# A routed expert layer: 32 experts over all tokens, against 39 (expert, tile) products over tokens sorted by expert

## The reference

```python
def _L2_ffn_ref(x, weight, scale, expert_masks, router_w):
    B, S, D_IN, D_OUT, E = (4, 128, 256, 256, 32)
    ...
    probs = jax.nn.softmax(jnp.einsum('bsd,ed->bse', x, router_w), axis=-1)
    top1_w, top1_idx = jnp.max(probs, axis=-1), jnp.argmax(probs, axis=-1)
    w_scaled = jnp.clip(jnp.round(weight / THRESH), -1.0, 1.0) * scale[:, None]
    def body(out, inputs):
        e_idx, mask_e = inputs
        y = jnp.einsum('bsi,oi->bso', x, w_scaled * mask_e)
        out = jnp.where((top1_idx == e_idx)[..., None], y * top1_w[..., None], out)
```

## Time and profile before

| | us |
|---|---|
| median of 3 runs | 1933.21 |
| lowest, highest | 1932.28, 1936.13 |
| the profiled execution, its time | 1934.06 |
| its span in the trace | 1932.3 |
| sublayer of the change: first router matmul to the first instruction of the epilogue | 1467.3 to 1608.2 |

### The profile page before, as it was taken

One profiled execution on the slowest core, in us unless ns is written; L12 is line 12 of the kernel. 1 busy time (PEld: TensorE's weight loads), 2 busy tenths in 40 slices (PEclk: granted clock), 3 DMA queues, 4 the chain that ended last, 5 costly groups with the idle time before them and its releaser, 6 DMA issues. The chain is left out here.

```text
span 1932.3 us, 32081 instructions
## 1 busy us (share of the span) xinstructions
PE 1599.6 (83%) x11620; PEld 1183.9 (61%) x11667; DVE 1422.6 (74%) x2379; ACT 790.1 (41%) x1245; POOL 529.3 (27%) x594
## 2 busy tenths in 40 slices
PE   7899999999898985566767678899995998889853
PEld 6678888887884662122546345688874884746631
DVE  3399999998666846899486764566685994668698
ACT  3367676666242635333234212533341002525522
POOL 2234444442342411776022003200000331314100
PEclk9899999999898987788969789999997999899975
DMA  3000000000000000000100020000001220010000
GB/s 148 28 28 27 27 27 26 23 27 6 12 1 13 3 8 36 0 0 0 47 4 2 28 109 4 12 18 12 12 19 57 74 65 31 2 58 2 2 1 22
DMA packets 18145, 49.24 MB, mean 25 GB/s; under 512 B 2035, under 2 KB 8436, under 8 KB 16886
## 3 DMA queue, kind: packets, MB, share of 16 engines
q1 hardware_dynamic: 18038, 47.78, 7.3%
HBM read 46.73 MB, written 1.05 MB: 25 GB/s over the span
## 5 line engine op out<-in xcount | busy, mean ns | idle before, releaser
L2124 DVE SCALAR_TENSOR_TENSOR arena<-psum,arena 128x1016 f32<-128x1016 f32 (+2 forms) x240 | 303.5, 1265 | 35.5 <-ACT arena L2061 29.8
L902 DVE TENSOR_REDUCE limits<-psum 128x4 f32<-128x512 f32 (+2 forms) x256 | 148.1, 620 | 81.9 <-PE psum L757 49.3
L1970 PE MATMUL psum<-ssm_XT_hi,ssm_split 128*128 128x512 f32 x640 | 194.2, 406 | 11.7 <-POOL ssm_split L1929 5.7
L870 ACT ACTIVATE PT<-psum 128x1024 f32<-128x1024 f32 x112 | 108.6, 1021 | 115.0 <-PE psum L788 115.0
L1970 PEld LDWEIGHTS psum<-ssm_XT_hi,ssm_split 128*128 128x128 f32 x640 | 115.9, 191 | 36.8 <-POOL ssm_split L1929 10.9
L2061 ACT ACTIVATE arena<-psum,arena 128x1024 f32<-128x1024 f32 x80 | 89.2, 1115 | 105.4 <-PE psum L1970 104.0
L2547 PE MATMUL psum<-expert,x 128*128 128x256 f16 x1024 | 114.0, 275 | 16.7 <-POOL expert L2533 16.7
L757 PE MATMUL psum<-K,QR 32*128 32x256 f32 (+1 forms) x320 | 118.3, 441 | 9.0 <-DVE limits L902 6.4
L2724 POOL TENSOR_TENSOR fed<-dtx,b_all 128x1024 f32<-128x1024 f32 x32 | 103.2, 3244 | 65.0 <-DVE state L2793 33.4
L2547 PEld LDWEIGHTS psum<-expert,x 128*128 128x128 f16 x1024 | 101.1, 99 | 29.5 <-issue 16.8
L2560 DVE SCALAR_TENSOR_TENSOR acc<-psum,gate_now,acc 128x256 f32<-128x256 f32 x256 | 111.9, 484 | 7.7 <-PE psum L2547 7.6
(11 more groups left out here) (443 smaller groups left out, 3850.0 us busy)
## 6 DMA issues: line engine op xcount, KB each, us to landing
expert_mask<-in_expert_masks SPq DMA_DIRECT2D x32, 256.0 KB, 2.6
arena<-in_ssm_in SPq DMA_DIRECT2D x16, 384.0 KB, 3.1
arena<-in_L_xattn SPq DMA_DIRECT2D x1, 5120.0 KB, 15.0
arena<-in_ssm_in SPq DMA_DIRECT2D x16, 256.0 KB, 3.0
arena<-in_L_ffn SPq DMA_DIRECT2D x1, 2592.0 KB, 9.0
arena<-in_L_xattn SPq DMA_DIRECT2D x2, 1280.0 KB, 9.5
arena<-in_L_ffn SPq DMA_DIRECT2D x1, 2176.0 KB, 8.2
ssm_gated<-in_ssm_z SPq DMA_DIRECT2D x4, 512.0 KB, 5.8
```

Of the source, the lines that this page charges most:

```text
L870: nc.scalar.activation(PT[:, u % 2, 2 * k:2 * k + 2, :, :].rearrange("p r h q -> p (r h q)"), p.psum[:, (2 + 2 * k) * 512:(4 + 2 * k) * 51 ...
L902: ins = nc.vector.tensor_reduce(limits[:, u % 2, r, :, k], score_bank(r)[:, :].rearrange("p (h k) -> p h k", h=4)[:, :, lo:hi], AX.X, ALU. ...
L1970: ins = nc.tensor.matmul(bank[tile_bank(r, tile) + half][:, :], w_part(tile, kw, c), x_part(kx, c, slice(half * 512, (half + 1) * 512)), s ...
L2124: ins = nc.vector.scalar_tensor_tensor(out[:, :, ago:], product[:, :, :P - ago], tap, out[:, :, ago:], ALU.mult, ALU.add)
```

## The change

The function is written anew; the rest of the program only moves by some lines. All is one block now.

The routing ends in a one-hot matrix (token x expert). Two matmuls over it count, for each tile and expert, the tokens up to each token and in all (the constants up_to and ones); a running sum over the counts (tensor_tensor_scan) gives each token its position among the tokens sorted by expert. Comparing these positions with 0 to 1023 gives a permutation matrix in float16, 8 tiles of 128 x 1024. TensorE multiplies the tokens by it: 8 x 8 matmuls of 128 x 512, which fill all 8 banks with the sorted, transposed tokens. ScalarE and VectorE copy four banks each to SBUF.

A sorted tile of 128 tokens holds only a few experts. Walking through sorted tokens, each step goes on either to the next expert or to the next tile, so 32 + 8 - 1 = 39 (expert, tile) pairs are enough. VectorE computes the list of pairs (finished, expert_at, index). In each step TensorE and VectorE read two numbers of the list from SBUF into registers (value_load) and use them as addresses. TensorE does 4 matmuls of 128 x 256 into one of four banks, VectorE adds the bank, times a 0/1 mask of the rows that belong to the pair, to the sum of that tile.

In the end the sum is split into two float16 parts again (ScalarE copies, VectorE subtracts), and 128 matmuls of 128 x 256 with the transposed permutation turn it back to the tokens' order. For that matrix, TensorE spreads the positions over the partitions (8 matmuls with ones, on a diagonal matrix that VectorE makes), ScalarE copies them out, and VectorE compares one tile after each fourth of the first 32 steps. VectorE then multiplies by probability and scale and adds to the tokens.

SP's loop over the masks is in the first block and starts right behind the next sublayer's weights. GpSimd multiplies the 32 masks one after the other, waiting for masks and for the ternary weight alone, and all 32 experts stay in SBUF. The sublayer's weights have two new tables, 0 to 1023 on all partitions and the row numbers.

```diff
--- before.py
+++ after.py
@@ -196,7 +196,8 @@
-        return [("router", rows(i[pre + "router_w"].T)), ("weight", rows(i[pre + "weight"].T)), ("scale", everywhere(i[pre + "scale"]))]
+        return [("router", rows(i[pre + "router_w"].T)), ("weight", rows(i[pre + "weight"].T)), ("scale", everywhere(i[pre + "scale"])),
+                ("positions", everywhere(np.arange(T, dtype=np.float32))), ("slots", np.arange(T, dtype=np.float32).reshape(B, P).T)]
...
@@ -2435,142 +2436,215 @@
...
-                with pe.Fori(0, trips) as i:
-                    for r in range(4):
-                        e = i * 4 + r
-                        pe.wait_ge(s.expert_ready.sem, s.expert_ready.at(e))
-                        for b in range(B):
-                            pe.wait_ge(s.product_taken.sem, s.product_taken.at(e * B + (b - B)))
-                            for part in range(2):
-                                for c in range(DC):
-                                    ins = nc.tensor.matmul(bank[b][:, :D], x16[:, part, c, b * P:(b + 1) * P], expert[:, r % 2, c, :],
-                                                           start=(part == 0 and c == 0), stop=(part == 1 and c == DC - 1))
-                            ins.then_inc(s.product_ready.up(trips), 1)
...
+    STEPS = E + B - 1
...
+            for e in range(E):
+                if e >= RING:
+                    sync.wait_ge(s.expert_ready.sem, s.expert_ready.at(e - RING))
+                sync.dma_start(mask[:, e % RING, :].rearrange("p (c n) -> p c n", c=DC), p.dram["expert_masks"][e]
+                               ).then_inc(mask_loaded[e % RING].up(16), 16)
...
+            pool.wait_ge(s.ternary_ready.sem, s.ternary_ready.at(0))
+            for e in range(E):
+                landed = mask_loaded[e % RING]
+                pool.wait_ge(landed.sem, landed.at(e // RING * 16 + 15))
+                nc.gpsimd.tensor_tensor(experts[:, e, :, :].rearrange("p c n -> p (c n)"), ternary[:, :], mask[:, e % RING, :], ALU.mult
+                                        ).then_inc(s.expert_ready.up(), 1)
...
+            pe.wait_ge(s.onehot_ready.sem, s.onehot_ready.at(0))
+            onehot = logits[:, :, :].rearrange("p b e -> p (b e)")
+            nc.tensor.matmul(bank[1][:, :B * E], p.c("up_to"), onehot, start=True, stop=True)
+            nc.tensor.matmul(bank[2][:, :B * E], p.c("ones"), onehot, start=True, stop=True).then_inc(s.counts_ready.up(), 1)
+            hold_clock(p, bank[7], 12)
+            pe.wait_ge(s.x16_ready.sem, s.x16_ready.at(1))
+            for b in range(B):
+                pe.wait_ge(s.perm_ready.sem, s.perm_ready.at(b))
+                for n, (part, c, half) in enumerate(tiles):
+                    ins = nc.tensor.matmul(bank[n][:, :], x16[:, part, b, c * P:(c + 1) * P], perm[:, b, half * 512:(half + 1) * 512],
+                                           start=(b == 0), stop=(b == B - 1))
+                    if b == B - 1:
+                        ins.then_inc(s.sorted_ready.up(), 1)
+            pe.wait_ge(s.diag_ready.sem, s.diag_ready.at(0))
+            pe.wait_ge(s.sorted_out_act.sem, s.sorted_out_act.at(3))
+            pe.wait_ge(s.sorted_out_dve.sem, s.sorted_out_dve.at(3))
+            for b in range(B):
+                ins = nc.tensor.matmul(bank[4 + b // 4][:, b % 4 * P:(b % 4 + 1) * P], p.c("ones"), diag[:, b, :], start=True, stop=True)
+            ins.then_inc(s.pos_psum.up(), 1)
+            pe.wait_ge(s.index_ready.sem, s.index_ready.at(0))
+            for i in range(STEPS):
+                e = pe.value_load(index[0:1, 0, i:i + 1], min_val=0, max_val=E - 1)
+                k = pe.value_load(index[0:1, 1, i:i + 1], min_val=0, max_val=B - 1)
+                pe.wait_ge(s.expert_ready.sem, s.expert_ready.at(min(i, E - 1)))
+                if i >= 4:
+                    pe.wait_ge(s.product_taken.sem, s.product_taken.at(i - 4))
+                for part in range(2):
+                    for c in range(DC):
+                        ins = nc.tensor.matmul(bank[i % 4][:, :D], sorted_x[:, bass.ds(k, 1), part, c, :].rearrange("p o t -> p (o t)"),
+                                               experts[:, bass.ds(e, 1), c, :].rearrange("p o n -> p (o n)"),
+                                               start=(part == 0 and c == 0), stop=(part == 1 and c == DC - 1))
+                ins.then_inc(s.product_ready.up(), 1)
...
+            pe.wait_ge(s.perm_turned.sem, s.perm_turned.at(B - 1))
...
+            for j in range(B // 2):
+                for half in range(2):
+                    b = 2 * j + half
+                    for k in range(B):
+                        for part in range(2):
+                            ins = nc.tensor.matmul(bank[4 + j][:, half * D:(half + 1) * D], perm[:, k, b * P:(b + 1) * P], acc16[:, part, k, :],
+                                                   start=(k == 0 and part == 0), stop=(k == B - 1 and part == 1))
+                ins.then_inc(s.y_ready.up(), 1)
...
+            nc.scalar.copy(x16[:, 0, :, :], p.X[:, :, :]).then_inc(s.x16_ready.up(), 1)
...
+            act.wait_ge(s.pos_psum.sem, s.pos_psum.at(0))
+            nc.scalar.copy(pos_row[:, :], p.psum[:, 4 * 512:6 * 512]).then_inc(s.pos_ready.up(), 1)
+            act.wait_ge(s.product_taken.sem, s.product_taken.at(STEPS - 1))
+            nc.scalar.copy(acc16[:, 0, :, :], acc[:, :, :]).then_inc(s.sum_split.up(), 1)
...
+            dve.wait_ge(s.x16_ready.sem, s.x16_ready.at(0))
+            nc.vector.tensor_tensor(x16[:, 1, :, :], p.X[:, :, :], x16[:, 0, :, :], ALU.subtract).then_inc(s.x16_ready.up(), 1)
...
+            then(nc.vector.tensor_copy(counts[:, :, :], bank[2][:, :B * E].rearrange("p (b e) -> p e b", b=B)))
+            then(nc.vector.tensor_tensor_scan(flat(cum), p.c("ones")[:, 0:1].broadcast_to([P, E * B]), flat(counts), 0.0, ALU.mult, ALU.add))
+            then(nc.vector.tensor_tensor(flat(base), flat(cum), flat(counts), ALU.subtract))
...
+            then(nc.vector.tensor_reduce(pos[:, :], chosen[:, :, :], AX.X, ALU.add))
...
+            for b in range(B):
+                nc.vector.tensor_scalar(perm[:, b, :], iota16[:, :], pos[:, b:b + 1], None, ALU.is_equal).then_inc(s.perm_ready.up(), 1)
+            for b in range(B):
+                ins = nc.vector.tensor_scalar(diag[:, b, :], p.c("ident"), pos[:, b:b + 1], None, ALU.mult)
...
+            then(nc.vector.tensor_tensor(finished[:, :, :], over_first(last_step[:, :], STEPS), over_last(positions[:, :STEPS], E), ALU.is_lt))
+            then(nc.vector.tensor_reduce(expert_at[:, 0, :], finished[:, :, :], AX.X, ALU.add))
...
+            nc.vector.tensor_copy(index[:, :, :], expert_at[:, :, :]).then_inc(s.index_ready.up(), 1)
...
+            for n in (1, 3, 5, 7):
+                dve.wait_ge(s.sorted_ready.sem, s.sorted_ready.at(n))
+                nc.vector.tensor_copy(sorted_tile(n), by_tile(n)).then_inc(s.sorted_out_dve.up(), 1)
...
+            for i in range(STEPS):
+                k = dve.value_load(index[0:1, 1, i:i + 1], min_val=0, max_val=B - 1)
+                at = dve.value_load(index[0:1, 2, i:i + 1], min_val=0, max_val=B * E - 1)
+                dve.wait_ge(s.product_ready.sem, s.product_ready.at(i))
+                if i:
+                    dve.wait_ge(s.product_taken.sem, s.product_taken.at(i - 1))
+                total_of = acc[:, bass.ds(k, 1), :].rearrange("p o n -> p (o n)")
+                nc.vector.scalar_tensor_tensor(total_of, bank[i % 4][:, :D], flat(chosen)[:, bass.ds(at, 1)], total_of, ALU.mult, ALU.add
+                                               ).then_inc(s.product_taken.up(), 1)
+                if i % 4 == 3 and i // 4 < B:
+                    if i == 3:
+                        dve.wait_ge(s.pos_ready.sem, s.pos_ready.at(0))
+                    nc.vector.tensor_scalar(perm[:, i // 4, :], pos_row[:, :], slots[:, i // 4:i // 4 + 1], None, ALU.is_equal
+                                            ).then_inc(s.perm_turned.up(), 1)
+            dve.wait_ge(s.sum_split.sem, s.sum_split.at(0))
+            nc.vector.tensor_tensor(acc16[:, 1, :, :], acc[:, :, :], acc16[:, 0, :, :], ALU.subtract).then_inc(s.sum_split.up(), 1)
...
+                dve.wait_ge(s.y_ready.sem, s.y_ready.at(j))
+                for half in range(2):
+                    ins = nc.vector.scalar_tensor_tensor(scaled[:, half, :], bank[4 + j][:, half * D:(half + 1) * D], top[:, 2 * j + half:2 * j + half + 1],
+                                                         p.w("scale"), ALU.mult, ALU.mult)
+                then(ins)
+                two = p.X[:, 2 * j:2 * j + 2, :]
+                then(nc.vector.tensor_tensor(two, two, scaled[:, :, :], ALU.add))
```

More of the change, by code:

```diff
@@ L2442, in masked_experts @@
     nc, s, bank = p.nc, p.s, p.bank
-    E = 32
+    E, RING = 32, 4
+    STEPS = E + B - 1
     mask_loaded = (s.mask_loaded0, s.mask_loaded1, s.mask_loaded2, s.mask_loaded3)
-    with ExitStack() as ctx:
+    with ExitStack() as ctx, nc.Block(no_gpsimd_drain=True) as block:
```

(32 more changed lines are left out.)

153 lines of the change are left out of this document (69 added, 84 removed).

## The result

The changed kernel takes 1947.1 us (median of 5 runs, 1944.07 to 1949.24), the kernel before 1932.32 (5 runs, 1931.79 to 1936.13): the ratio is 1.0073, with a 95% interval of 1.0059 to 1.0087. It is slower by 14.8 us, where 7 us less were forecast. The profiled execution took 1948.91, with a span of 1947.1.

The account below looks back on a forecast made before the run. PE and DVE were taken to bound the old loop together. Preparation 33 plus port 29 (62), loop 49.5 and end 22.5 gave a sublayer of 134 against 140.9 us, so 1926 us; 8-in-10 range 1892 to 1955.

Parts of the forecast that it names:

- preparation, undisturbed: From the router's first matmul to the first listed product, with no port waits: 33 us.
- the shared port: In the preparation, DVE instructions wait for GpSimd's running product: 29 us added, lower end 0, upper end 33.
- 39 listed products: The loop: 39 steps of 1.27 us on PE, 49.5 us, with 0.35 per register load.
- end: After the loop: splitting the sum, 128 matmuls turning back, last scalings and addition, into the epilogue: 22.5 us.
- the part on the loop: PE's step as two loads at 0.35, register instructions 0.37 and matmul issue 0.2: 1.27 us.
- The first rival: In the preparation the port costs little, 0 to 12 us instead of 29; 1897 to 1909 us, chance 0.2.
- The second rival: Register loads bound the loop by round trips, 0.67 us each; step 1.9, loop 74, 1951 us; chance 0.28.
- The third rival: Loop loads as cheap as register instructions, 0.05 to 0.15 us; step 0.67 to 0.87, 1903 to 1911 us; chance 0.12.
- DVE's step beside PE's: In the loop DVE's step is as long as PE's and runs beside it; PSUM waits cost nothing.
- The signs named ahead: Trace marks: GpSimd product spacing, slowed small DVE instructions, first listed product near 62, products 1.27 apart, slow-clock turning back.
- The case that came: Slower kernel: register loads bound the loop's 39 steps, sublayer 159 us, 1951 us; chance 0.28.
- its likeliest case: Port at full price in the preparation, loop loads of 0.25 to 0.43 us: 1926, range 1918 to 1933, chance 0.35.

Follow-up runs that it names:

- E1: The changed kernel with GpSimd waiting to start its 32 products until the list of steps is ready; 1926.94 us, ratio 0.9965 to the kernel before.
- E2: The changed kernel without the range checks of the values loaded into registers, loads kept; 1923.51 us, ratio 0.9938 to the kernel before.
- E8: The changed kernel with GpSimd's 32 products replaced by fills with ones that read nothing, masks left out; 1927.74 us, one execution.
- E4: The changed kernel with each step's pair from a fixed list known at build, no loads or checks; 1899.78 us, ratio 0.9817 to the kernel before.
- E6: E1 with one packed number loaded per step and taken apart in registers, no checks; 1896.72 us, ratio 0.981 to the kernel before.

## Why the prediction was wrong

Counted from the router's first matmul, forecast and measured:

| stretch | forecast | measured | difference |
|---|---|---|---|
| preparation, undisturbed | 33 | 32.4 (E1) | -0.6 |
| the shared port | 29 | 23.2 (changed kernel less E1) | -5.8 |
| 39 listed products | 49.5 | 76.5 | +27.0 |
| end | 22.5 | 22.9 | +0.4 |
| sublayer | 134 | 155.0 | +21.0 |

1926 and 21 are 1947. The step that failed is in the part on the loop: "on PE 2x2 behind the loads and 4 before the matmuls, at 0.046 0.37", and "With 0.2 for the matmuls' own issue". The number of instructions was right, their price not. The row 0.046 is of SP's additions to one register, an instruction of one kind, and its duration without the gaps to its neighbours. Measured: 0.3 for each check with its gaps (E2 took two away and the step fell by 0.6), 0.58 for four matmuls with computed addresses, and 0.11 for the semaphore. That is 1.28, where 0.37 + 0.2 = 0.57 had been meant to pay for all of it. The load itself, on which the forecast spent its care and its rivals, was 0.36 with its gap against 0.35: right.

- **The port.** The mechanism was right and shown by E1 and E8: it is instructions of the kinds named, 31 of the 34, and what they wait for is GpSimd's running one. It cost 23.2, not 29. The forecast charged a whole product, 1.17, for 28 waits; the 31 waits measured are 0.20 to 0.97, 0.77 in the mean. The earlier trace rows had said so: there the scan grows by 2.02 and GpSimd's product by 1.93, less than the other's 2.34 and 2.26, which the forecast read as "just the other's length". The first rival (0 to 12) is refuted.
- **The second rival** gave 0.67 per load, a step of 1.9, a sublayer of 159 and 1951. Its number came (0.66 per load with its check, 1.98, 155.0, 1947.1) and its statement was right that the sequencer's time for register values bounds the loop. Its reason was not: no round trip of 0.67, but 0.36 of load with its gap, and 0.3 of check. That its number came is luck. The floor of about 600 ns for a tensor_load, from the Trainium skill ("DMA: Bandwidth & Descriptors", section "Latency and other measured facts"), is not met here: 0.30 for one register, 0.53 for two; the measurement decides. The 1946 that was worked out from it came near by luck as well.
- **The third rival** (cheap loads) is refuted by 0.30.
- **DVE's step beside PE's** was right: DVE waited for PE 38 times of 39, and the four banks were enough (E2).
- **The end** was right, 22.9 against 22.5. Its last term, 0.5 into the epilogue, is 0.74 in the earlier trace rows (1605.14 + 2.29 to 1608.17).
- **The signs named ahead**: GpSimd's products at 1.17 to 1.6 apart (42.31 / 32 = 1.32) and the turning back at the low clock for its start (granted 0.50 for 4.1 us) were seen. The small DVE instructions were slower, but most take 0.56 to 1.10 where 1.2 to 1.6 was named, and the first listed product came at 55.6, not near 62. "Products are 1.5 or more apart" was named as what would show the forecast wrong, and it was that.

The case that came had a chance of 0.28, and 1947.1 lies inside the range of 1892 to 1955. An error of 0.1 us per load or check counts 78 times on PE, 8 us, more than the whole gain of 7; the sum was too near to nothing for its likeliest case to tell the sign.

What stays open: why E4's median shows 4 us less than its sublayer, why the waits for the port have the lengths they have, and why a second register in one load costs 0.23.

## What to carry to other kernels

A loop over a computed list pays its engines' sequencers per step, whatever the products cost: count loads, checks, semaphores and computed addresses on each engine (here 0.36, 0.3, 0.11 and 0.15 us apiece with their gaps), and set the sum beside the busy time saved; leave checks out where the list's making bounds it, and load one number rather than two. Work that GpSimd does ahead of need is not free while VectorE is the chain: here its start moved behind VectorE's preparation gave back 20 us at no cost, since a step needs one expert at most. A busy share of half on every engine, with idle time put down to "issue" or to a semaphore long since given, is how a loop bound by its own instructions looks.

## What was not expected of the hardware

- A register load from SBUF is 0.30 us on PE's and on DVE's queue, and 0.53 for two registers. A bounds comparison is 0.151 on PE and 0.183 on DVE. With its assertion and the gaps behind both it is about 0.3 of PE's step (E2).
- Taking a number apart by 32 in registers costs 0.15 in one instruction on PE (E6), against 0.05 to 0.08 for the others there.
- Eight float16 comparisons of 128x1024 on DVE take 3.26 alone (0.41 apart), 10.45 beside GpSimd's products, 4.54 beside its fills.
- Two queues that both want the port take turns: 24.0 us of waits over 31 instructions, while GpSimd's own products grow from a median of 1.16 (E1, beside the listed products) to 1.34.
